# First-layer attention of a decoder: the order of work in one turn, rearranged into two halves on TensorE, ScalarE and VectorE

## The chip, the cores and the metric

One core of a Trainium2 chip runs the whole kernel in one launch. Times are microseconds of that core. A number is the median of several executions or, where a profile is read, belongs to the one execution that was profiled.

## The reference

The kernel computes a two-layer decoder on 4 sequences of 512 tokens with 128 features. Each layer is an attention, a cross-attention and a mixture of experts, each with a layer norm ahead and a residual addition behind. The change lies in the first part of the first layer alone:

```python
q = jnp.einsum('bsf,hfd->bhsd', x, wq)      # x is the layer norm of the input
k = jnp.einsum('bsf,hfd->bhsd', x, wk)
v = jnp.einsum('bsf,hfd->bhsd', x, wv)      # B = 4, S = 512, H = 16 heads of DK = 64
scores = jnp.einsum('bhsd,bhtd->bhst', q, k) / sqrt(DK)
attn = jax.nn.softmax(scores, axis=-1)
out = jnp.einsum('bhst,bhtd->bhsd', attn, v)
x = x_in + out.transpose(0, 2, 1, 3).reshape(B, S, H * DK) @ wo
```

The later parts, among them the second layer's attention with relative positions, are computed by other lines of the same program (`a1_...`), after this one.

## The kernel before, in words

The kernel is written by hand: each engine has its own program, all of them meet through semaphores, and each engine works strictly through its list. Nothing but the written order and the waits decides when a thing runs.

**Turns.** The first attention is a loop of 32 turns. Turn g is one pair of heads of one sequence (8 pairs by 4 sequences). A turn has four query tiles p of 128 tokens, and in each tile two heads, so eight units u = 0 to 7, where u = 2p + head. The first turn, the second and the last are written apart (`first`, `second`, `last`); those between run in a loop of two turns, since buffers with the index `par` alternate.

**What TensorE does in turn g** (`a0_turn` in the tensor block, line 1035):
- `a0_scores(g, p)`, line 991: six matmuls of 64 rows by 512 columns. Queries and keys are each split into a high and a low part, and three products of parts are added, for two heads. The heads lie in the two halves of the rows and run in pairs. They write banks 0 and 1 for even tiles, 2 and 3 for odd ones. Tile p waits for the exponentials that read these banks last (`a0_exp`).
- `a0_turn_t(g, u)`, line 1006: the transposes of unit u's probabilities, four of 128 by 128, into bank 4 for even u, bank 5 for odd. It waits for the normalisation of unit u (`a0_norm`) and for the copy of the unit that was in its bank before (`a0_tcd`, VectorE, or `a0_tca`, ScalarE). The transposes of units 4 to 7 are made in the turn after.
- `a0_values(g - 1, half)`, line 1014: 16 matmuls of 64 columns each that make half of the previous turn's output in bank 7. It needs all copies of that half, and its first half waits until the addition before it has read the bank (`a0_x`).
- `a0_project_q`, `_k`, `_v` of turn g + 1, lines 973 to 989. All three write bank 6, so K waits until Q has been read by both readers (`a0_ql`), V until K has (`a0_kl`), and the next Q until V has (`a0_vc`).
- `a0_output(g - 1)`, line 1028: the product with `wo`, from the copied features (`a0_ftc`) into bank 7.

**What the others do.** VectorE takes the negated maximum of every unit's scores (`a0_maximum`, line 1569), copies even units' transposes (`a0_copy`, 1564), takes the reciprocal of the sum (`a0_reciprocal`, 1578), makes the low parts of Q and K (`a0_low_q`, `a0_low_k`, 1582 to 1589) and adds the output to X (`a0_add`, 1573). ScalarE makes the exponentials (`a0_exp_of`, 737) with the sum in an accumulator, and waits for the transpose of the unit four before, whose probabilities lie in the same buffer; it copies the odd units' transposes (`a0_copy`, 732), Q, K and V out of bank 6 (716 to 726) and the features out of bank 7 (728). GpSimd multiplies each unit's probabilities by the reciprocal (563), in the order of units. SP copies the next pair's weights and the layer norm's output into `wst` and `hst` once the V projection is done (line 417), 32 times; in the first eight turns it also issues the loads of later weights.

**The order before.** TensorE's turn has four equal steps. With (u) for a transpose, those of 4 to 7 and the values belonging to the turn before:

```
p=0: scores 0, (4), (5), values 0, Q     p=1: scores 1, (6), (7), K
p=2: scores 2, (0), (1), values 1        p=3: scores 3, (2), (3), V, output
```

Of the kernel before, what the change touches and what calls it, by code (L numbers as in the profile page):

```python
# [23 lines left out]
QT = SEQ // P  # L24
# [77 lines left out]
def decoder_kernel(nc, a, out):  # L102
    ctx = ExitStack()
    with ctx:
# [254 lines left out]
        PAIRS = B * HP  # L359
        STACK = 16 * 3 * HQ  # L360
        UN = 2 * QT
# [321 lines left out]
        def _(act):  # L683
# [32 lines left out]
            def a0_copy_q(g, par):  # L716
                act.wait_ge(a0_q, g + 1)
                act.activation(a0_qk[par][:, 0, :], bank[6][:, :], ACT.Copy, scale=float(DK) ** -0.5).then_inc(a0_qc, 1)  # L718

            def a0_copy_k(g, par):  # L720
                act.wait_ge(a0_k, g + 1)
                act.activation(a0_qk[par][:, 2, :], bank[6][:, :], ACT.Copy).then_inc(a0_kc, 1)

            def a0_copy_v(g, par):
                act.wait_ge(a0_v, g + 1)
                act.activation(a0_vtok[par], bank[6][:, :].rearrange("p (a b) -> p a b", a=QT), ACT.Copy).then_inc(a0_vc, 1)

            def a0_copy_feats(g):
                act.wait_ge(a0_pv, g * 2 + 2)
                act.activation(featsT[:, :], bank[7][:, :], ACT.Copy).then_inc(a0_ftc, 1)  # L730

            def a0_copy(g, u, par):
                act.wait_ge(a0_t, g * UN + u + 1)
                act.activation(a0_pT[par][1][:, :, (u // 2) * P:(u // 2 + 1) * P],
                               bank[5][:, :].rearrange("p (a b) -> p a b", a=QT), ACT.Copy).then_inc(a0_tca, 1)

            def a0_exp_of(g, u, first):
                act.wait_ge(a0_max, g * UN + u + 1)
                if not (first and u < 4):
                    act.wait_ge(a0_t, g * UN + u - 3)  # L740
                act.activation(a0_p[u % 4], bank[u % 4][:, :], ACT.Exp, bias=negmax[:, u:u + 1],  # L741
                               accum_out=den[:, u:u + 1]).then_inc(a0_exp, 1)

            def a0_turn(g, par, first, last):
                for p in range(QT):
                    a0_exp_of(g, 2 * p, first)
                    a0_exp_of(g, 2 * p + 1, first)
                    if p < 2:
                        if not first:
                            a0_copy(g - 1, 2 * p + 5, 1 - par)  # L750
                    else:
                        a0_copy(g, 2 * p - 3, par)
                    if not last:
                        if p == 0:
                            a0_copy_q(g + 1, 1 - par)
                        if p == 1:
                            a0_copy_k(g + 1, 1 - par)
                        if p == 3:
                            a0_copy_v(g + 1, 1 - par)
                    if p == 2 and not first:  # L760
                        a0_copy_feats(g - 1)

            a0_copy_q(0, 0)
            a0_copy_k(0, 0)
# [183 lines left out]
        def _(pe):  # L948
# [31 lines left out]
            def a0_project_k(g):  # L980
                pe.wait_ge(a0_ql, g + 1)
                pe.matmul(bank[6][:, :], wst[:, 1, :], hst[:, :], start=True, stop=True).then_inc(a0_k, 1)
# [8 lines left out]
            def a0_scores(g, p, par, first):  # L991

                if p == 0:
                    pe.wait_ge(a0_ql, g + 1)
                    pe.wait_ge(a0_kl, g + 1)
                if not (first and p < 2):
                    pe.wait_ge(a0_exp, g * UN + 2 * p - 2)
                for i, (q, k) in enumerate(((0, 2), (0, 3), (1, 2))):
                    for h in range(2):
                        r = h * DK  # L1000
                        mm = pe.matmul(bank[2 * (p % 2) + h][:, :], a0_qk[par][r:r + DK, q, p * P:(p + 1) * P],  # L1001
                                       a0_qk[par][r:r + DK, k, :], start=(i == 0), stop=(i == 2))
                        if i == 2:
                            mm.then_inc(a0_s, 1)
# [28 lines left out]
                mm.then_inc(a0_o, 1)  # L1033

            def a0_turn(g, par, first, last, second=False):
                for p in range(QT):
                    a0_scores(g, p, par, first)
                    for u in (2 * p - 4, 2 * p - 3):
                        if u >= 0:
                            a0_turn_t(g, u, first)  # L1040
                        elif not first:
                            a0_turn_t(g - 1, u + UN, False)
                    if p == 0:
                        if not first:
                            a0_values(g - 1, 1 - par, 0, second)
                        if not last:
                            a0_project_q(g + 1)
                    if p == 1 and not last:
                        a0_project_k(g + 1)
                    if p == 2 and not first:  # L1050
                        a0_values(g - 1, 1 - par, 1, second)
                    if p == 3:
                        if not last:
                            a0_project_v(g + 1)
                        if not first:
                            a0_output(g - 1)

            a0_project_q(0)
            a0_project_k(0)
# [5 lines left out]
                a0_turn(i * 2 + 1, 1, False, False)  # L1065
            a0_turn(PAIRS - 2, 0, False, False)
            a0_turn(PAIRS - 1, 1, False, True)
            a0_values(PAIRS - 1, 1, 0, False)
            for u in range(4, UN):
                a0_turn_t(PAIRS - 1, u, False)  # L1070
            a0_values(PAIRS - 1, 1, 1, False)
            a0_output(PAIRS - 1)

# [70 lines left out]
            for t in range(1, NT + 4):  # L1144
# [5 lines left out]
                u = (t - 3) // 2  # L1150
# [330 lines left out]
            with pe.Fori(0, E1 // 2) as i:  # L1481
                for k in range(8):
# [4 lines left out]
                    for hf in range(2):  # L1487
                        u = 2 * k + hf
# [16 lines left out]
        def _(dve):  # L1505
# [82 lines left out]
                dve.wait_ge(a0_kc, g + 1)  # L1588
                dve.tensor_tensor(a0_qk[par][:, 3, :], bank[6][:, :], a0_qk[par][:, 2, :].bitcast(F32), ALU.subtract).then_inc(a0_kl, 1)

            def a0_turn(g, par, first, last):
                for p in range(QT):
                    a0_maximum(g, 2 * p)
                    a0_maximum(g, 2 * p + 1)
                    if p >= 2:
                        a0_copy(g, 2 * p - 4, par)
                    elif not first:
                        a0_copy(g - 1, 2 * p + 4, 1 - par)
                    a0_reciprocal(g, 2 * p)
                    a0_reciprocal(g, 2 * p + 1)  # L1600
                    if not last:
                        if p == 0:
                            a0_low_q(g + 1, 1 - par)
                        if p == 1:
                            a0_low_k(g + 1, 1 - par)
                    if p == 3 and not first:
                        a0_add(g - 1)

            a0_low_q(0, 0)
            a0_low_k(0, 0)  # L1610
            a0_turn(0, 0, True, False)
            with dve.Fori(0, PAIRS // 2 - 1) as i:
                a0_turn(i * 2 + 1, 1, False, False)
                a0_turn(i * 2 + 2, 0, False, False)
            a0_turn(PAIRS - 1, 1, False, True)
            a0_copy(PAIRS - 1, 4, 1)
            a0_copy(PAIRS - 1, 6, 1)
            a0_add(PAIRS - 1)
# [557 lines left out]
```

## Time and profile before

| what | value |
|---|---|
| time, median of 3 (lowest to highest) | 1595.6 us (1595.15 to 1600.68) |
| the profiled execution | 1596.56 us, of which 1594.8 us from its first to its last instruction |
| TensorE matmuls busy | 1379.0 us, 86% of the span |
| TensorE weight loads busy | 959.2 us, 60% |
| VectorE busy | 999.3 us, 63% |
| ScalarE busy | 724.2 us, 45% |
| GpSimd busy | 540.8 us, 34% |
| granted TensorE clock, mean | 0.925 |
| bytes moved | 61.36 MB, mean 38 GB/s |

The first attention runs from 46.6 us (first scores, line 1001) to about 542 us (last output, line 1031), nearly a third of the span. The page's second part shows the span in 40 slices of 39.9 us:

```
PE   4899999999999789714389759989999999949998
DVE  2566666666666677487033338697787778646554
ACT  2566666666666455300023234454654655523222
POOL 1455555555555200100711255432433434121110
PEclk9999999999999999755789879999999999959999
```

Each digit is a tenth of a slice, 9 being 90% or more; the stage is in slices 2 to 14. How to read it: a matmul's printed duration reaches to the modelled end of its result, so matmuls behind each other overlap in print, and their pace is seen in the distances of their starts. A busy share of TensorE near one says that there is always a matmul under way, not that the array works at its peak. What stands in brackets behind a row is idle time of that engine ahead of it, and what released it.

### The profile page before, as it was taken

To read this page: it belongs to the slowest core of one execution; us is meant where nothing else is said; L and a number is where in the kernel's file an instruction comes from. 1 tells how busy PE (TensorE), PEld (TensorE's weight loads), DVE (VectorE), ACT (ScalarE), POOL (GpSimd) and SP (SyncE) were. 2 spreads that over 40 slices of the span, in tenths; PEclk is the share of its full clock that TensorE was granted. 3 is DMA by queue.
4 is the path that set the end of the run, shared out by engine and by line. 5 is a ranking of instruction groups with operands and counts; after the bars stand their busy time and mean duration, and the time that the engine had idled before them with its cause. 6 is when DMAs were issued, how large, how long until landed. Compare 5 with 4: busy or idle time off the path is not lost.

```text
span 1594.8 us, 30921 instructions
## 1 busy us (share of the span) xinstructions
PE 1379.0 (86%) x10918; PEld 959.2 (60%) x10918; DVE 999.3 (63%) x2407; ACT 724.2 (45%) x1467; POOL 540.8 (34%) x548
## 2 busy tenths in 40 slices
PE   4899999999999789714389759989999999949998
PEld 2566666666666456512167436666766776638887
DVE  2566666666667677487033338697787778646554
ACT  2566666666666455300023234454654655523222
POOL 1455555555555200100711255432433434121110
PEclk9999999999999999755789879999999999959999
DMA  3333011010010200000023123211111211000000
GB/s 131 96 95 109 24 34 35 23 35 33 24 35 23 60 1 1 1 1 1 16 73 91 29 58 108 44 46 30 39 48 29 46 45 41 7 0 1 0 0 26
DMA packets 91918, 61.36 MB, mean 38 GB/s; under 512 B 26841, under 2 KB 78890, under 8 KB 91830
## 3 DMA queue, kind: packets, MB, share of 16 engines
q1 hardware_dynamic: 89782, 58.88, 13.3%
q0 software_dynamic: 2048, 1.27, 0.3%
q8 instruction: 59, 0.97, 0.2%
q14 instruction: 29, 0.24, 0.0%
HBM read 21.63 MB, written 10.49 MB: 20 GB/s over the span
## 4 chain that ended last, share of the span: by engine, by line
PE 75%; DVE 15%; issue 3%; ACT 3%; another core or an unknown queue 2%; SPq 1%; DMA 1%; POOL 0%; DVEq 0%; ACTq 0%
PE psum L1011 8%; PE psum L1024 8%; PE psum L1001 7%; PE psum L1372 7%; PE psum L1494 6%; PE psum L1363 5%; PE psum L1384 4%; PE psum L1476 4%; PE psum L1357 3%; PE psum L1219 2%; PE psum L978 2%; PE psum L987 2%; DVE negmax L1987 2%; PE psum L1031 2%
## 5 line engine op out<-in xcount | busy, mean ns | idle before, releaser
L563 POOL TENSOR_TENSOR arena<-arena,rden 128x512 f32<-128x512 f32 x256 | 260.8, 1040 | 255.3 <-DVE rden L1580 255.3
L741 ACT ACTIVATE arena<-psum,negmax 128x512 f32<-128x512 f32 x256 | 173.6, 683 | 136.0 <-DVE negmax L1571 134.8
L1987 DVE TENSOR_REDUCE negmax<-psum 128x1 f32<-128x512 f32 x256 | 165.2, 685 | 75.9 <-PE psum L1363 69.4
L1571 DVE TENSOR_REDUCE negmax<-psum 128x1 f32<-128x512 f32 x256 | 164.3, 683 | 11.1 <-PE psum L1001 7.5
L1011 PE MATMUL psum<-cst,arena 128*128 128x128 f32 x1024 | 144.0, 280 | 1.6 <-DVE arena L1566 0.7
L1011 PEld LDWEIGHTS psum<-cst,arena 128*128 128x128 f32 x1024 | 109.0, 141 | 53.0 <-issue 51.5
L1001 PE MATMUL psum<-a_qk 64*128 64x512 f32 x768 | 124.5, 429 | 0.0
L1363 PE MATMUL psum<-w,wqkv 128*64 128x208 f32 x1024 | 124.0, 364 | 0.0
L623 POOL TENSOR_TENSOR a_qblk<-a_qstack,cst 96x512 fp32r<-96x512 f32 x64 | 68.6, 1073 | 136.7 <-PE psum L1363 127.8
L1357 PE MATMUL psum<-a_kstack,a_qblk 96*128 96x512 f32 x256 | 97.8, 464 | 16.7 <-DMA a_kstack<-a_klo 16.7
L1001 PEld LDWEIGHTS psum<-a_qk 64*128 64x128 f32 x768 | 62.8, 186 | 69.9 <-issue 59.1
L894 ACT ACTIVATE kT<-psum,negmax 128x512 f32<-128x512 f32 x64 | 44.0, 687 | 125.3 <-PE psum L1372 84.7
L1494 PE MATMUL psum<-f_h,f_w 128*128 128x512 f32 x384 | 99.2, 407 | 1.5 <-DVE arena L2075 0.8
L1363 PEld LDWEIGHTS psum<-w,wqkv 128*64 128x64 f32 x1024 | 64.5, 141 | 58.3 <-issue 48.8
L1991 DVE COPY arena<-psum 128x512 f32<-128x512 f32 x128 | 87.1, 680 | 2.3 <-PE psum L1372 2.3
L894 ACT ACTIVATE hst<-psum,negmax 128x512 f32<-128x512 f32 x64 | 44.0, 687 | 94.6 <-PE psum L1372 47.1
L931 ACT ACTIVATE arena<-psum 128x512 f32<-128x512 f32 x64 | 38.2, 597 | 104.3 <-PE psum L1494 104.3
L1494 PEld LDWEIGHTS psum<-f_h,f_w 128*128 128x128 f32 x384 | 70.5, 191 | 18.9 <-DVE arena L2075 3.5
L888 ACT ACTIVATE arena<-psum 128x512 f32<-128x512 f32 x128 | 76.1, 595 | 1.6 <-PE psum L1372 1.6
L2075 DVE TENSOR_TENSOR arena<-psum,arena 128x512 f32<-128x512 f32 x64 | 44.2, 691 | 47.4 <-ACT arena L931 47.3
L1384 PE MATMUL psum<-arena,w 128*32 128x128 f32 x2048 | 65.5, 276 | 4.5 <-issue 3.6
L1584 DVE SCALAR_TENSOR_TENSOR a_qk<-psum,a_qk 128x512 fp32r<-128x512 f32 x32 | 22.1, 691 | 74.2 <-ACT a_qk L718 74.2
(303 smaller groups left out, 2779.8 us busy)
## 6 DMA issues: line engine op xcount, KB each, us to landing
hst<-hT SPq DMA_DIRECT2D x32, 256.0 KB, 2.3
a_kstack<-a_khi SPq DMA_DIRECT2D x128, 64.0 KB
wst<-wqkv SPq DMA_DIRECT2D x32, 192.0 KB, 2.4
w<-in_ew SPq DMA_DIRECT2D x2, 2048.0 KB, 8.6
a_kstack<-a_klo SPq DMA_DIRECT2D x64, 64.0 KB
xs_rows<-f SPq DMA_DIRECT2D x3, 1024.0 KB, 5.6
arena<-xs_rows SPq DMA_DIRECT2D x8, 384.0 KB, 3.7
ys_rows<-wqkv SPq DMA_DIRECT2D x8, 384.0 KB, 2.7
```

The source lines that it names most:

```text
L563: pool.tensor_tensor(a0_p[u % 4], a0_p[u % 4], rden[:, u:u + 1].broadcast_to([P, SEQ]), ALU.mult).then_inc(a0_norm, 1)
L741: act.activation(a0_p[u % 4], bank[u % 4][:, :], ACT.Exp, bias=negmax[:, u:u + 1], accum_out=den[:, u:u + 1]).then_inc(a0_exp, 1)
L1001: mm = pe.matmul(bank[2 * (p % 2) + h][:, :], a0_qk[par][r:r + DK, q, p * P:(p + 1) * P], a0_qk[par][r:r + DK, k, :], start=(i == 0), stop ...
L1011: mm = pe.transpose(bank[4 + u % 2][:, kt * P:(kt + 1) * P], a0_p[u % 4][:, kt * P:(kt + 1) * P], ident)
L1024: mm = pe.matmul(bank[7][h * DK:(h + 1) * DK, qs], a0_vtok[par][:, kt, h * DK:(h + 1) * DK], a0_pT[par][h][:, kt, qs], start=(kt == 0), st ...
L1357: pe.matmul(bank[n % 4][:, :], qblk[:, hg, j, lg:lg + 2, :, :].rearrange("p g h l -> p (g h l)"), kstack[it % 2][:, n // 4, :], start=True ...
L1363: mm = pe.matmul(bank[n % 4][blk * HQ * LG:(blk + 1) * HQ * LG, first_key:first_key + WIN], rblk[:, hg, j, g, :, :].rearrange("p h l -> p ...
L1372: mm = pe.transpose(bank[4 + n % 2][:, kt * P:(kt + 1) * P], ptile[n % 4][:, kt * P:(kt + 1) * P], ident)
L1384: mm = pe.matmul(bank[6][32 * j:32 * j + 32, grp * P:(grp + 1) * P], vst[:, kt, hg * HG + grp * 4 + j, :], a1_pT(hg, kt, grp, j), start=(k ...
L1494: mm = pe.matmul(bank[2 * (u % 2) + w][:, :], w_parts[:, e, wp, w * FF + hf * P:w * FF + (hf + 1) * P], h_parts[hp][:, c * SEQ:(c + 1) * S ...
L1571: dve.tensor_reduce(negmax[:, u:u + 1], bank[u % 4][:, :], AX.X, ALU.max, negate=True).then_inc(a0_max, 1)
L1987: dve.tensor_reduce(negmax[:, n % 8:n % 8 + 1], bank[n % 4][:, :], AX.X, ALU.max, negate=True).then_inc(a1_max, 1)
```

## The change

The bodies of the three turns are written out anew, with the same instructions in another order. Scores of tiles 0 and 1 follow each other, and so do those of tiles 2 and 3. Transposes, values and projections stand between these pairs:

```
first half:  scores 0, scores 1, output of turn g-2, (4), (5), values 0, Q, (6), (7), K
second half: scores 2, scores 3, (0), (1), values 1, (2), (3), V
```

The output and the addition to X are a turn later than before, behind the first two score tiles; two outputs come behind the last turn, and there the transposes 4 and 5 precede the first half of the values, 6 and 7 the second. ScalarE's and VectorE's orders follow. ScalarE's is now exponentials 0, 1, copy 5, Q, exponentials 2, 3, copy 7, K, exponential 4, copy 1, exponential 5, features, exponential 6, copy 3, exponential 7, V. VectorE's loop now also has the second turn written apart. GpSimd's and SP's programs are not changed. The helper functions that issue instructions are not changed either.

```diff
--- before.py
+++ after.py
@@ -742,23 +742,28 @@
                                accum_out=den[:, u:u + 1]).then_inc(a0_exp, 1)
 
             def a0_turn(g, par, first, last):
-                for p in range(QT):
-                    a0_exp_of(g, 2 * p, first)
-                    a0_exp_of(g, 2 * p + 1, first)
-                    if p < 2:
-                        if not first:
-                            a0_copy(g - 1, 2 * p + 5, 1 - par)
-                    else:
-                        a0_copy(g, 2 * p - 3, par)
-                    if not last:
-                        if p == 0:
-                            a0_copy_q(g + 1, 1 - par)
-                        if p == 1:
-                            a0_copy_k(g + 1, 1 - par)
-                        if p == 3:
-                            a0_copy_v(g + 1, 1 - par)
-                    if p == 2 and not first:
-                        a0_copy_feats(g - 1)
+                a0_exp_of(g, 0, first)
+                a0_exp_of(g, 1, first)
+                if not first:
+                    a0_copy(g - 1, 5, 1 - par)
+                if not last:
+                    a0_copy_q(g + 1, 1 - par)
+                a0_exp_of(g, 2, first)
+                a0_exp_of(g, 3, first)
+                if not first:
+                    a0_copy(g - 1, 7, 1 - par)
+                if not last:
+                    a0_copy_k(g + 1, 1 - par)
+                a0_exp_of(g, 4, first)
+                a0_copy(g, 1, par)
+                a0_exp_of(g, 5, first)
+                if not first:
+                    a0_copy_feats(g - 1)
+                a0_exp_of(g, 6, first)
+                a0_copy(g, 3, par)
+                a0_exp_of(g, 7, first)
+                if not last:
+                    a0_copy_v(g + 1, 1 - par)
 
             a0_copy_q(0, 0)
             a0_copy_k(0, 0)
@@ -1033,27 +1038,31 @@
                 mm.then_inc(a0_o, 1)
 
             def a0_turn(g, par, first, last, second=False):
-                for p in range(QT):
-                    a0_scores(g, p, par, first)
-                    for u in (2 * p - 4, 2 * p - 3):
-                        if u >= 0:
-                            a0_turn_t(g, u, first)
-                        elif not first:
-                            a0_turn_t(g - 1, u + UN, False)
-                    if p == 0:
-                        if not first:
-                            a0_values(g - 1, 1 - par, 0, second)
-                        if not last:
-                            a0_project_q(g + 1)
-                    if p == 1 and not last:
-                        a0_project_k(g + 1)
-                    if p == 2 and not first:
-                        a0_values(g - 1, 1 - par, 1, second)
-                    if p == 3:
-                        if not last:
-                            a0_project_v(g + 1)
-                        if not first:
-                            a0_output(g - 1)
+                a0_scores(g, 0, par, first)
+                a0_scores(g, 1, par, first)
+                if not (first or second):
+                    a0_output(g - 2)
+                if not first:
+                    a0_turn_t(g - 1, 4, second)
+                    a0_turn_t(g - 1, 5, second)
+                    a0_values(g - 1, 1 - par, 0, second)
+                if not last:
+                    a0_project_q(g + 1)
+                if not first:
+                    a0_turn_t(g - 1, 6, second)
+                    a0_turn_t(g - 1, 7, second)
+                if not last:
+                    a0_project_k(g + 1)
+                a0_scores(g, 2, par, first)
+                a0_scores(g, 3, par, first)
+                a0_turn_t(g, 0, first)
+                a0_turn_t(g, 1, first)
+                if not first:
+                    a0_values(g - 1, 1 - par, 1, second)
+                a0_turn_t(g, 2, first)
+                a0_turn_t(g, 3, first)
+                if not last:
+                    a0_project_v(g + 1)
 
             a0_project_q(0)
             a0_project_k(0)
@@ -1065,9 +1074,12 @@
                 a0_turn(i * 2 + 1, 1, False, False)
             a0_turn(PAIRS - 2, 0, False, False)
             a0_turn(PAIRS - 1, 1, False, True)
+            a0_output(PAIRS - 2)
+            a0_turn_t(PAIRS - 1, 4, False)
+            a0_turn_t(PAIRS - 1, 5, False)
             a0_values(PAIRS - 1, 1, 0, False)
-            for u in range(4, UN):
-                a0_turn_t(PAIRS - 1, u, False)
+            a0_turn_t(PAIRS - 1, 6, False)
+            a0_turn_t(PAIRS - 1, 7, False)
             a0_values(PAIRS - 1, 1, 1, False)
             a0_output(PAIRS - 1)
 
@@ -1588,31 +1600,46 @@
                 dve.wait_ge(a0_kc, g + 1)
                 dve.tensor_tensor(a0_qk[par][:, 3, :], bank[6][:, :], a0_qk[par][:, 2, :].bitcast(F32), ALU.subtract).then_inc(a0_kl, 1)
 
-            def a0_turn(g, par, first, last):
-                for p in range(QT):
-                    a0_maximum(g, 2 * p)
-                    a0_maximum(g, 2 * p + 1)
-                    if p >= 2:
-                        a0_copy(g, 2 * p - 4, par)
-                    elif not first:
-                        a0_copy(g - 1, 2 * p + 4, 1 - par)
-                    a0_reciprocal(g, 2 * p)
-                    a0_reciprocal(g, 2 * p + 1)
-                    if not last:
-                        if p == 0:
-                            a0_low_q(g + 1, 1 - par)
-                        if p == 1:
-                            a0_low_k(g + 1, 1 - par)
-                    if p == 3 and not first:
-                        a0_add(g - 1)
+            def a0_turn(g, par, first, last, second=False):
+                a0_maximum(g, 0)
+                a0_maximum(g, 1)
+                if not (first or second):
+                    a0_add(g - 2)
+                a0_maximum(g, 2)
+                a0_maximum(g, 3)
+                if not first:
+                    a0_copy(g - 1, 4, 1 - par)
+                a0_reciprocal(g, 0)
+                a0_reciprocal(g, 1)
+                if not last:
+                    a0_low_q(g + 1, 1 - par)
+                if not first:
+                    a0_copy(g - 1, 6, 1 - par)
+                a0_reciprocal(g, 2)
+                a0_maximum(g, 4)
+                a0_reciprocal(g, 3)
+                a0_maximum(g, 5)
+                a0_copy(g, 0, par)
+                if not last:
+                    a0_low_k(g + 1, 1 - par)
+                a0_maximum(g, 6)
+                a0_maximum(g, 7)
+                a0_reciprocal(g, 4)
+                a0_reciprocal(g, 5)
+                a0_copy(g, 2, par)
+                a0_reciprocal(g, 6)
+                a0_reciprocal(g, 7)
 
             a0_low_q(0, 0)
             a0_low_k(0, 0)
             a0_turn(0, 0, True, False)
-            with dve.Fori(0, PAIRS // 2 - 1) as i:
+            a0_turn(1, 1, False, False, second=True)
+            with dve.Fori(1, PAIRS // 2 - 1) as i:
+                a0_turn(i * 2, 0, False, False)
                 a0_turn(i * 2 + 1, 1, False, False)
-                a0_turn(i * 2 + 2, 0, False, False)
+            a0_turn(PAIRS - 2, 0, False, False)
             a0_turn(PAIRS - 1, 1, False, True)
+            a0_add(PAIRS - 2)
             a0_copy(PAIRS - 1, 4, 1)
             a0_copy(PAIRS - 1, 6, 1)
             a0_add(PAIRS - 1)
```

## Rows read from the trace of the kernel before

**Rows 1.** Chain that ended last, shares by line, from the page.

```profile
PE psum L1011 8%; PE psum L1024 8%; PE psum L1001 7%; PE psum L1372 7%; PE psum L1494 6%; PE psum L1363 5%; PE psum L1384 4%; PE psum L1476 4%; PE psum L1357 3%; PE psum L1219 2%; PE psum L978 2%; PE psum L987 2%; DVE negmax L1987 2%; PE psum L1031 2%
```

**Rows 2.** Windows view; busy of PE, PEld, DVE, ACT, POOL; clock; DMA.

```profile
250.00:300.00 50.00, 50.00 (x352) 32.25 (x352) 34.16 (x76) 31.80 (x78) 26.12 (x26) 1.00 0.08 28
```

**Rows 3.** Chain in order of time, first and last of 53 pieces.

```profile
109.10 1.88 PE psum L1024 x16
...
505.60 1.88 PE psum L1024 x16
```

**Rows 4.** Timeline, TensorE, one turn; start us, us, what.

```profile
306.21 1.09 PE L1011 MATMUL psum<-cst,arena 128*128 128x128 f32 x8
307.24 1.95 PE L1024 MATMUL psum<-arena,vtok 128*64 128x256 f32 x16
309.11 1.12 PE L978 MATMUL psum<-hst,wst 128*128 128x512 f32 x2
310.17 0.97 PE L1001 MATMUL psum<-a_qk 64*128 64x512 f32 x6
311.07 1.09 PE L1011 MATMUL psum<-cst,arena 128*128 128x128 f32 x8
312.00 1.02 PE L982 MATMUL psum<-hst,wst 128*128 128x512 f32 x2
312.95 0.96 PE L1001 MATMUL psum<-a_qk 64*128 64x512 f32 x6
...
318.74 1.06 PE L987 MATMUL psum<-wst,hst 128*128 128x128 f32 x8
319.63 1.06 PE L1031 MATMUL psum<-wqkv,featsT 128*128 x8
320.62 0.96 PE L1001 MATMUL psum<-a_qk 64*128 64x512 f32 x6
```

**Rows 5.** Timeline, TensorE, narrow windows that begin inside a group.

```profile
310.50 0.63 PE L1001 MATMUL psum<-a_qk 64*128 64x512 f32 x4
310.74 0.40 PE L1001 MATMUL psum<-a_qk 64*128 64x512 f32 x2
...
311.23 0.93 PE L1011 MATMUL psum<-cst,arena 128*128 128x128 f32 x7
```

**Rows 6.** Timeline, all engines, the stage's first turn.

```profile
50.16 1.10 PE L978 MATMUL psum<-hst,wst 128*128 128x512 f32 x2 [2.04 <-issue]
...
51.29 0.60 ACT L718 ACTIVATE a_qk<-psum 128x512 fp32r<-128x512 f32 x1 [0.97 <-PE psum L978]
51.92 0.69 DVE L1584 SCALAR_TENSOR_TENSOR a_qk<-psum,a_qk 128x512 fp32r<-128x512 f32 x1 [1.40 <-ACT a_qk L718]
52.74 0.50 PEld L982 LDWEIGHTS psum<-hst,wst 128*128 128x128 f32 x2 [0.65 <-DVE a_qk L1584]
```

**Rows 7.** Timeline, a steady turn's addition, then the last turn.

```profile
320.90 0.69 DVE L1576 TENSOR_TENSOR X<-X,psum 128x512 f32 x1 [0.62 <-PE psum L1031]
...
532.13 0.67 DVE L1576 TENSOR_TENSOR X<-X,psum 128x512 f32<-128x512 f32 x1
...
532.95 1.95 PE L1024 MATMUL psum<-w,arena 128*64 128x256 f32 x16 [1.22 <-DVE X L1576]
...
534.83 1.09 PE L1011 MATMUL psum<-cst,arena 128*128 128x128 f32 x8
535.52 0.69 DVE L1566 COPY w<-psum 128x512 f32<-128x512 f32 x1 [2.72 <-PE psum L1011]
```

**Rows 8.** Timeline, ScalarE, a steady turn.

```profile
313.07 0.68 ACT L741 ACTIVATE arena<-psum,negmax 128x512 f32<-128x512 f32 x1
313.64 0.20 ACT L741 ACTIVATION_READ_ACCUMULATOR arena<-psum,negmax 128x1 f32 x1
313.73 0.60 ACT L734 ACTIVATE arena<-psum 128x512 f32<-128x512 f32 x1
314.21 0.60 ACT L722 ACTIVATE a_qk<-psum 128x512 fp32r<-128x512 f32 x1
```

## The prediction

> **What bounds the kernel now.** I read the shares of the chain that ended last first: three of its largest entries, lines 1011, 1024 and 1001, are TensorE lines of the first layer's attention, the only stage that the diff touches [rows 1]. The second layer's attention with relative positions is in later lines, which the diff leaves alone: its cost is nothing, and a change that was meant for it has not been made there. The next view is the busy time in a stretch of the stage: TensorE is busy for all 50 us at a granted clock of 1.00, VectorE, ScalarE and GpSimd for 34, 32 and 26 [rows 2]. So the stage runs at TensorE's own pace. The chain's pieces give that pace: the first and the last of 53 values groups, two to a turn, lie 396.50 us apart, which is 26 turns of 15.25 us [rows 3].
>
> The timeline of one turn shows what the pace is made of [rows 4]. I write S for the six score matmuls of a query tile, T for the transposes of two units (head and tile), V for a half of the values, Q, K and P for the projections of query, key and value, O for the output; T(u) is unit u's transpose. What counts is the step from the start of one group to the start of the next; the printed durations overlap. S is 0.90, T 0.93 ahead of K and 1.03 ahead of V, V 1.87, Q 1.06, K 0.95, P 0.89, O 0.99.
>
> **A change of form costs time.** S uses 64 rows of the array, V 64 columns, all others the whole [rows 4]. P and O are eight equal matmuls each, and only O is followed by another form: leaving costs 0.10. Q and K do the same work, both leave, and only Q follows another form: entering costs 0.11. Narrow views of S and T say the same: the pairs of S start 0.33, 0.24 and 0.33 apart (the last to the T behind), so 0.09 goes at each end, and T's first step is 0.16 where the seven behind it take 0.77, or 0.11 each: entering costs T 0.05 [rows 5]. Entering V was part of V before and still is.
>
> **The turn without waits.** The new order is S S O T V Q T K, S S T V T P. It has eight changes of form, the old one eleven.
> - S S: 0.33 + 4 x 0.24 + 0.33 = 1.62, taken as 1.61 since 0.24 is rounded up; twice 3.22. Two separate pairs cost 3.60 before.
> - O behind S: 0.89 + 0.11 = 1.00. T(4), T(5) behind O, ahead of V: 8 x 0.11 + 0.10 = 0.97.
> - V 1.87 twice; the one step from V to T that rows show, 532.95 to 534.83, is 1.88 [rows 7], so I take 1.88.
> - Q ahead of T, no leaving: 0.96. T(6), T(7) between Q and K: 0.87. K 0.95.
> - T(0), T(1) between S and V 1.03; T(2), T(3) behind V 0.93; P, now leaving to S, 0.99.
> The sum is 3.22 + 1.00 + 0.97 + 3.76 + 0.96 + 0.87 + 0.95 + 1.03 + 0.93 + 0.99 = 14.68, which is 0.57 less than 15.25. Were that all, the change would give back 17 us. No arithmetic is added or removed, no DMA; SP's staging starts behind P as before; O, S, T and V lay between P's end and Q, 4.8 us, now S S O T V do, 5.5, so its two DMAs land no later relative to Q.
>
> **The wait at K.** K writes the bank of Q, so it waits until ScalarE has copied Q and VectorE has taken the low part. In the old turn S and T stand between Q and K: 312.00 - 309.11 = 2.89 [rows 4]. In the new one only T(6), T(7) do: 0.96 + 0.87 = 1.83. What the chain needs is seen in the kernel's first turn, where too little stood between them: Q starts at 50.16, the copy at 51.29, the low part at 51.92, and the load for K at 52.74, its idle time put down to that low part: 2.58 [rows 6]. TensorE stands for 0.75, and K has a cold start, worth an entry, 0.11: 0.86 a turn. It isn't hidden: all that stands behind K in the queue, the whole second half, moves with it. On ScalarE the copy of Q now stands ahead of the exponentials of units 2 and 3, on VectorE the low part ahead of copy 6; they have until the second half, over 2 us later.
>
> **The wait at V.** The output moved to follow the scores, and the values behind it write the bank that VectorE's addition to X reads. Addition starts 1.27 after a warm O starts [rows 4, 7], so 1.38 after one that enters; from its start to the values it releases is 0.82 (532.13 to 532.95) [rows 7]. Needed 2.20, filled by O and T 1.97: 0.23 a turn. In VectorE's queue the maxima of units 2 and 3 stand behind this addition and come 1 us later than they could; the score tiles that need their banks are 5 us off. Before, the addition had four groups' time and cost nothing.
>
> **The wait at the second S.** It writes the banks of units 6 and 7, so it needs exponential 7. That reuses unit 3's probabilities and stands in ScalarE's queue behind exponential 6, which needs T(2), and copy 3. From T(2)'s start: 0.69 to its first reader (534.83 to 535.52) [rows 7], then 0.66 from an exponential to a copy, 0.48 from a copy to the next, 0.77 to the end of the accumulator's read [rows 8], 0.13 from an end to TensorE's start (52.61 to 52.74) [rows 6]: 2.73. TensorE needs 0.93 + 0.99 + 0.81 for T, P and the first S: 2.73 too. Between 0 and 0.3 (were a step slower, with the cold start); I take 0.05, nearer the lower end, as every step is measured.
>
> Other releases come early by this reckoning: GpSimd's normalisations, 26 of 50 us busy [rows 2], get units 0 to 3 over 2 us ahead of their transposes; exponentials 0 and 1 now wait for T(4) and T(5) until about 3 us into the turn, and what needs them comes after 9.
>
> **The sum.** 14.68 + 0.86 + 0.23 + 0.05 = 15.82, so 0.57 a turn longer; over 29 steady turns +16.5. The ends: turn 1 has no O and no addition to wait for, 1.23 less, so -0.7 against before; the first turn takes its second S earlier, -0.4; the tail has its transposes ahead of the values, so that copies run beside them, an estimate of -1.1. Together +14.3. The profiled execution took 1596.56 (span 1594.8): 1610.9. It stands 1.0 over the median of 1595.6, so for a median I say 1610.
>
> **The rivals.** A change of this kernel can be told from none from about 0.5%, 8 us, on.
> - Forecast: the K wait and most of the two others, 1604 to 1616. Chance 0.60.
> - Only K waits, or the drains saved are some tenths larger: 14.68 + 0.86 = 15.54, 29 x 0.29 - 2.2 = +6, so 1602. For it: the addition's start rests on one latency, and the last wait is even. Against: the addition is a plain chain of measured steps. Chance 0.14.
> - Faster: the Q to K chain is covered after all, and only the drains count. It decides at K: with the other waits in place the turn is equal to the old one when Q to K takes about 2.0, and 1.83 with no other wait gives -17 and the ends: 1577. For it: TensorE is the only full engine [rows 2] and three changes of form are really gone. Against: 2.58 is measured with ScalarE and VectorE idle ahead of the two steps [rows 6], and nothing in the diff shortens a step. Chance 0.09.
> - The last wait grows: the exponentials of the second half have only T(2) to P to run in, and if a ScalarE step there takes 0.3 more, with it every turn: +9, so 1619. For it: the sum is even, with no slack. Chance 0.12.
> - The two S side by side save nothing, since the second tile's weights can't load while both row halves still stream: then each joint costs what it did, 0.18, or 0.36 a turn, and the time is 1620. Against: inside S the third pair's loads are hidden at 0.24 with both halves in flight [rows 5]. Chance 0.05. The Trainium skill, "TensorE: Matmul & The Clock Gate", Part 3, states a rule for it: weight loads overlap matmuls in flight only where the row group differs. By that rule 0.24 could not be; the trace doesn't agree inside a group, and at a joint no row shows it.
>
> **How the numbers follow.** The time is the forecast's. The range of 1600 to 1618 takes in the K-only case and the forecast's bounds; outside are the covered chain and the upper parts of the last two. Slower by over 0.5%: forecast, the grown wait, the joint, 0.77; within: 0.14; faster: 0.09.
>
> **What would show it.** In the changed profile: turns of about 15.8, two score groups as one of x12 over 1.6 us; idle time of TensorE of about 0.75 ahead of line 982's matmuls, put down to the low part of Q, and about 0.2 ahead of the first values, put down to the addition; busy below 50 of 50 in the stretch, clock still 1.00; lines of later stages unchanged. No idle time at K, or a turn under 15.3, proves me wrong.

## The result, and the profile after

The changed kernel takes 1608.3 us, the median of 13 runs (1603.82 to 1616.56), the kernel before 1595.6 us, the median of 13 (1590.78 to 1603.16). The ratio is 1.0072, with a 95% interval of 1.0054 to 1.0089: slower by 12.7 us. The forecast was 1610, in 1600 to 1618.

The chain in order of time of the changed kernel, the first and the last of 51 values groups, answers to [rows 3]:

```profile
104.83 1.88 PE psum L1029 x16
...
500.28 1.88 PE psum L1029 x16
```

They lie 395.45 us apart, which is 25 turns of 15.82 us. Before it was 15.25, and 15.82 was forecast. The busy time in the stretch of [rows 2] (columns as there):

```profile
250.00:300.00 50.00, 47.83 (x345) 32.74 (x344) 31.69 (x73) 31.95 (x78) 27.04 (x28) 1.00 0.08 28
```

TensorE is no longer busy throughout, its clock is still 1.00, and it issues 345 matmuls in 50 us where it issued 352. The timeline of TensorE over one turn, answering to [rows 4]:

```profile
300.10 1.16 PE L1036 MATMUL psum<-wqkv,featsT 128*128 x8
301.09 1.04 PE L1016 MATMUL psum<-cst,arena 128*128 128x128 f32 x8
302.32 1.95 PE L1029 MATMUL psum<-w,arena 128*64 128x256 f32 x16 [0.19 <-DVE X L1588]
304.20 1.12 PE L983 MATMUL psum<-hst,wst 128*128 128x512 f32 x2
305.16 1.04 PE L1016 MATMUL psum<-cst,arena 128*128 128x128 f32 x8
306.74 1.13 PE L987 MATMUL psum<-hst,wst 128*128 128x512 f32 x2 [0.54 <-DVE a_qk L1596]
307.79 1.66 PE L1006 MATMUL psum<-a_qk 64*128 64x512 f32 x12
309.39 1.09 PE L1016 MATMUL psum<-cst,arena 128*128 128x128 f32 x8
310.41 1.95 PE L1029 MATMUL psum<-w,arena 128*64 128x256 f32 x16
312.29 1.09 PE L1016 MATMUL psum<-cst,arena 128*128 128x128 f32 x8
313.22 1.06 PE L992 MATMUL psum<-wst,hst 128*128 128x128 f32 x8
314.20 1.79 PE L1006 MATMUL psum<-a_qk 64*128 64x512 f32 x12
315.92 1.16 PE L1036 MATMUL psum<-wqkv,featsT 128*128 x8
```

Three places are to be seen, in the letters of the prediction.
- **K.** From T(6), T(7) at 305.16 to K at 306.74 it is 1.58 where the transposes alone take 0.87: TensorE stands for 0.71, and its idle time is put down to VectorE's low part of Q. K's own step is 1.05 (306.74 to 307.79), 0.10 over a warm K's 0.95. Together 0.81.
- **V.** From T(4), T(5) at 301.09 to the values at 302.32 it is 1.23, against 0.97 without a wait: 0.26, put down to the addition to X.
- **The second S.** The pair of tiles at 314.20 takes 1.72 to the next group, the pair at 307.79 takes 1.60: 0.12.

The sum is 1.19 us a turn, and 15.82 - 1.19 leaves 14.63 for a turn without waits, 0.62 less than the old turn of 15.25. About 0.5 of it comes of fewer changes of form and of scores side by side, the rest of a short wait in the old turn, shown further down. The waits take it all and more. The timeline of the other engines shows the chain behind K's wait, answering to [rows 6]:

```profile
305.36 0.60 ACT L718 ACTIVATE a_qk<-psum 128x512 fp32r<-128x512 f32 x1 [1.69 <-PE psum L983]
...
305.99 0.69 DVE L1596 SCALAR_TENSOR_TENSOR a_qk<-psum,a_qk 128x512 fp32r<-128x512 f32 x1 [1.89 <-ACT a_qk L718]
...
306.74 0.30 PEld L987 LDWEIGHTS psum<-hst,wst 128*128 128x128 f32 x2 [0.78 <-DVE a_qk L1596]
```

Q starts at 304.20, K at 306.74: 2.54, where the first turn of the kernel before took 2.58. ScalarE and VectorE both stood idle ahead of their step, so neither is late: it is the chain itself that is long. And the last wait, on the load side of TensorE and on ScalarE:

```profile
314.20 0.69 ACT L741 ACTIVATE arena<-psum,negmax 128x512 f32<-128x512 f32 x1
314.77 0.21 ACT L741 ACTIVATION_READ_ACCUMULATOR arena<-psum,negmax 128x1 f32 x1
...
315.03 0.53 PEld L1006 LDWEIGHTS psum<-a_qk 64*128 64x128 f32 x6 [0.27 <-ACT arena L741]
```

Exponential 7 starts at 314.20, its accumulator is read by 314.98, and the loads for the second tile start at 315.03, 0.83 behind the first tile.

**Where the stage ends.** The last output of the kernel before and of the changed one, each a line of TensorE's timeline (the window of the second ends before the last of its eight matmuls):

```profile
540.83 1.16 PE L1031 MATMUL psum<-wqkv,featsT 128*128 128x128 f32 x8 [0.69 <-ACT featsT L730]
```

```profile
557.12 1.05 PE L1036 MATMUL psum<-wqkv,featsT 128*128 128x128 f32 x7 [0.69 <-ACT featsT L730]
```

The stage ends 16.3 us later. The profiled execution took 1616.56 us, the highest of the 13 and 20.0 more than the one before, so 3.7 came later. They lie in one stretch of the second layer's attention, here in the windows view of the kernel before and then of the changed one:

```profile
1100.00:1120.00 20.00, 19.79 (x185) 13.84 (x183) 15.65 (x34) 11.27 (x20) 7.01 (x7) 1.00 0.20 50
```

```profile
1116.00:1136.00 20.00, 19.79 (x147) 13.31 (x145) 12.88 (x27) 8.48 (x14) 3.75 (x4) 0.74 0.20 50
```

The same work ran at a mean granted clock of 0.74 instead of 1.00, so half of that stretch at the lower of the two levels, and got through 147 matmuls instead of 185. The change touches nothing there, and runs of one and the same kernel lie up to 13 us apart. I read totals to some 4 us, therefore, and turns to hundredths.

### The profile page after: what moved, and what is told of

Its sections match the earlier page's. It is cut to its first block, busy times and chain, and to the rows that moved or that the text cites. A ratio compares the mean times of both kernels' runs of the same rounds, so it can differ in the third digit from the quotient of the medians.

```text
span 1614.8 us, 30925 instructions
## 1 busy us (share of the span) xinstructions
PE 1377.8 (85%) x10918; PEld 976.0 (60%) x10918; DVE 994.3 (62%) x2407; ACT 728.8 (45%) x1467; POOL 541.5 (34%) x548
## 4 chain that ended last, share of the span: by engine, by line
PE 72%; DVE 17%; ACT 3%; issue 3%; another core or an unknown queue 2%; SPq 1%; DMA 1%; DVEq 0%; POOL 0%; ACTq 0%
PE psum L1029 8%; PE psum L1384 7%; PE psum L1006 7%; PE psum L1506 6%; PE psum L1375 5%; PE psum L1016 4%; PE psum L1396 4%; PE psum L1488 4%; PE psum L1369 3%; PE psum L987 2%; PE psum L983 2%; PE psum L1231 2%; PE psum L1036 2%; DVE negmax L2014 2%; PE psum L992 2%
## 5 line engine op out<-in xcount | busy, mean ns | idle before, releaser
L1016 PEld LDWEIGHTS psum<-cst,arena 128*128 128x128 f32 x1024 | 113.6, 141 | 41.4 <-issue 39.8
L1016 PE MATMUL psum<-cst,arena 128*128 128x128 f32 x1024 | 136.6, 276 | 0.4 <-DVE arena L1578 0.4
L1006 PE MATMUL psum<-a_qk 64*128 64x512 f32 x768 | 113.0, 424 | 0.3 <-ACT arena L741 0.3
L1006 PEld LDWEIGHTS psum<-a_qk 64*128 64x128 f32 x768 | 66.3, 189 | 47.1 <-ACT arena L741 32.6
L626 POOL TENSOR_TENSOR wqkv<-big_k,cst 128x512 f32<-128x512 f32 x64 | 67.6, 1056 | 0.0
```

The source lines that it names most:

```text
L1016: mm = pe.transpose(bank[4 + u % 2][:, kt * P:(kt + 1) * P], a0_p[u % 4][:, kt * P:(kt + 1) * P], ident)
```

## The experiments

Each turn length below is read from the chain as above, from two of its values groups a whole number of turns apart. Times are medians, each beside runs of the kernel before on the same chip. The turns came out within 0.1 us of what was expected, but for K ahead of transposes (0.25 more). All eight totals came out above, by 2.5 to 8 us. Against the kernel before, they differ from 29 times the change of the turn by 1.1 less to 4.4 more, so the theories are judged by the turns.

### The price of a change of form

The kernel before, with the V projection between the two halves of the second values group:

```diff
                 for kt in range(QT):
+                    if kt == 2 and between:
+                        between()
                     for h in range(2):
...
-                        a0_values(g - 1, 1 - par, 1, second)
+                        a0_values(g - 1, 1 - par, 1, second, None if last else lambda: a0_project_v(g + 1))
                     if p == 3:
-                        if not last:
+                        if first:
                             a0_project_v(g + 1)
```

> The kernel before with the V projection put between the two halves of the 16 matmuls of the second values group, so that two changes of form are added (values to projection, projection to values) and no instruction and no wait. Theory (a change of form costs 0.15 to 0.2 us): turn 15.25 + 0.36 = 15.6 us, time 1595.6 + 11 = 1607. Rival (form costs nothing, what is saved by side-by-side scores is something of the scores alone): 15.25 us, 1596.

1611.2 us, ratio 1.0076 (1.0046 to 1.0106). The chain, 24 turns apart, then TensorE's timeline:

```profile
108.23 1.88 PE psum L1026 x16
...
482.49 1.88 PE psum L1026 x16
```

```profile
303.00 1.08 PE L1026 MATMUL psum<-w,arena 128*64 128x256 f32 x8
304.01 1.16 PE L987 MATMUL psum<-wst,hst 128*128 128x128 f32 x8
305.10 1.08 PE L1026 MATMUL psum<-w,arena 128*64 128x256 f32 x8
306.12 0.96 PE L1001 MATMUL psum<-a_qk 64*128 64x512 f32 x6
```

The turn is 15.59 us, 0.34 more: 0.17 for each of two changes, with no new wait. The parts show it: the two halves of V take 1.01 and 1.02, together 0.15 over one V of 1.88, and P takes 1.09, 0.20 over its 0.89. The rival that form costs nothing falls.

### The wait at K, made in the kernel before

The same wait without anything else of the change: K ahead of transposes 6 and 7 instead of behind them.

```diff
                 for p in range(QT):
                     a0_scores(g, p, par, first)
+                    if p == 1 and not last:
+                        a0_project_k(g + 1)
                     for u in (2 * p - 4, 2 * p - 3):
...
-                    if p == 1 and not last:
-                        a0_project_k(g + 1)
```

> The kernel before with the key projection ahead of transposes 6 and 7 instead of behind them, nothing else. Theory: Q to K takes 2.6 us, and only Q and one score tile, 1.96 us, stand between them, so TensorE stands for 0.64 with about 0.05 for the cold start: turn 15.25 + 0.69 = 15.9 us, time 1595.6 + 31 x 0.69 = 1617. Rival (the transposes' own short waits, 0.13 us a turn, are absorbed by it): 15.8, 1613. Rival (the K wait is hidden): 15.25, 1596.

1624.9 us, ratio 1.0158 (1.0115 to 1.0200). TensorE's timeline:

```profile
210.70 0.96 PE L1001 MATMUL psum<-a_qk 64*128 64x512 f32 x6
212.18 1.12 PE L982 MATMUL psum<-hst,wst 128*128 128x512 f32 x2 [0.52 <-DVE a_qk L1584]
...
215.00 0.66 PE L1011 MATMUL psum<-cst,arena 128*128 128x128 f32 x4
215.86 0.63 PE L1011 MATMUL psum<-cst,arena 128*128 128x128 f32 x4 [0.20 <-ACT w L734]
```

The turn is 16.15 us (24 turns from 127.08 to 514.68 in its chain), 0.90 more, where I had 0.69. The K wait is near the expected 0.64: 1.48 from S to K instead of 0.90, 0.58. The rest is mostly a wait that I had expected to be absorbed: T(7) moved 0.96 nearer to T(1), which needs its bank, and the copy between them stands on ScalarE behind two exponentials. T(0), T(1) take 1.42 here (215.00 to 216.42), 1.18 and 1.11 in two turns of the kernel before, and 1.03 with no wait. A K wait in an otherwise old turn costs what the chain says, and a moved group also moves what its bank's next user waits for.

### K behind the scores, in the changed kernel

```diff
-                if not last:
-                    a0_project_k(g + 1)
                 a0_scores(g, 2, par, first)
                 a0_scores(g, 3, par, first)
+                if not last:
+                    a0_project_k(g + 1)
```

> The changed kernel with the key projection moved from ahead of the scores of tiles 2 and 3 to behind them. Theory (the K wait costs 0.8 us a turn because too little stands between Q and K): TensorE's idle time ahead of K is gone, but the third-tile scores then reach exponential 3 early. That exponential stands behind the copy of Q: in the changed kernel's trace the load of Q starts at 304.20, exponential 3 starts at 306.52 and its read ends at 307.30, 3.1 us behind Q, while tile 3's scores would now come 2.7 us behind it. So a wait of about 0.5 with a cold start takes the place of the 0.8: turn about 15.5 us against 15.82, time about 1599. Rival (the copy and the low part are hidden and the turn is long for another reason): turn stays at 15.8, 1608. Rival (nothing takes its place): turn 15.0, 1584.

1605.5 us, ratio 1.0052 (1.0029 to 1.0075). TensorE's timeline:

```profile
312.45 0.97 PE L1006 MATMUL psum<-a_qk 64*128 64x512 f32 x6
313.67 0.96 PE L1006 MATMUL psum<-a_qk 64*128 64x512 f32 x6 [0.26 <-ACT arena L741]
```

The turn is 15.58 (24 turns from 121.64 to 495.64 in its chain), 0.24 less than the changed kernel's. K no longer waits, and tile 3's scores do: 1.22 from tile 2's instead of the 0.81 of three unstalled pairs, put down to an exponential. So 0.81 was removed and 0.57 came back in its place. 0.51 of that is this wait and its restart (tiles 2 and 3 take 2.11, where an unstalled pair takes 1.60), since exponential 3 stands behind the copy of Q on ScalarE; the other 0.06 is K's entry, which is dearer than the transposes'. The K wait hid this one in the changed kernel.

### The output back at the end of the turn

```diff
-                if not (first or second):
-                    a0_output(g - 2)
...
                 if not last:
                     a0_project_v(g + 1)
+                if not first:
+                    a0_output(g - 1)
```

The addition goes with it, to the end of VectorE's turn.

> The changed kernel with the output and the addition to X back at the end of the turn, behind the V projection. Theory (the values wait for the addition 0.24 us a turn, the second score tile 0.1 for exponential 7, and the output behind scores pays an entry of 0.06 more than a transpose does): idle time ahead of the first values goes, the second tile's scores come 0.9 us later behind exponential 7 and don't wait, the K wait stays at 0.8. Turn 15.82 - 0.24 - 0.12 - 0.05 = 15.4 us, time about 1597. Rival (these are small and the K wait takes up whatever they give): turn 15.8, 1608.

1603.1 us, ratio 1.0037 (1.0014 to 1.0060).

The turn is 15.38 (24 turns from 138.06 to 507.26 in its chain), 0.44 less than the changed kernel's; 0.26 of it is the wait for the addition, 0.12 the one for exponential 7, the rest the warmer entries. The K wait was untouched: Q to K takes 2.54 (309.08 to 311.62 in its timeline). The place of the output and the place of Q each cost by themselves.

### Exponential 7 ahead of copy 3

```diff
                 a0_exp_of(g, 6, first)
-                a0_copy(g, 3, par)
                 a0_exp_of(g, 7, first)
+                a0_copy(g, 3, par)
```

> The changed kernel with exponential 7 ahead of copy 3 on ScalarE, nothing else. Theory (the second score tile waits for exponential 7, 0.12 us a turn with its restart): the chain from T(2) to the end of exponential 7 is shorter by a copy's step of 0.48, so the wait goes: turn 15.82 - 0.12 = 15.70 us, time 1608 - 4 = 1604. Rival (the later copy 3 makes transpose 5 or the V copy late): turn 15.8 or more, 1608. Nothing changes at K or at the first values.

The second pair of tiles in TensorE's timeline:

```profile
308.98 1.66 PE L1006 MATMUL psum<-a_qk 64*128 64x512 f32 x12
310.56 1.16 PE L1036 MATMUL psum<-wqkv,featsT 128*128 x8
```

The turn is 15.68 (24 turns from 124.59 to 500.94 in its chain), 0.14 less, and the pair takes 1.58 instead of 1.72: the wait is named rightly. The total doesn't show it: 1611.2 us, ratio 1.0087 (1.0065 to 1.0110), overlaps with that of the changed kernel. 4 us are less than what the rest of the kernel varies by.

### Q ahead of the values: the version that keeps the gain

If both large waits come of too little work behind a start, one move mends both: Q one place earlier puts V behind Q, and puts Q between O and V.

```diff
                     a0_turn_t(g - 1, 5, second)
-                    a0_values(g - 1, 1 - par, 0, second)
                 if not last:
                     a0_project_q(g + 1)
+                if not first:
+                    a0_values(g - 1, 1 - par, 0, second)
```

> The changed kernel with the query projection one place earlier on TensorE, behind transposes 4 and 5 and ahead of the first values. Theory (both large waits come of too little work behind a start): between Q and K then stand V, T(6) and T(7), 3.8 us against the 2.6 needed, and between O and V stand T and Q, 2.9 against 2.2, so both waits go. The changes of form stay eight. Exponential 3 ends about 6.1 us behind the transposes' start, tile 3's scores come at 6.5. Turn 14.63 + 0.12 for the second score tile = 14.75 us, time 1595.6 - 30 x 0.5 - 2 = 1578. Rival: Q now stands 3.6 us behind the end of the V projection, and the copy of the layer norm's output into its buffer lands about 3.5 us behind it; if it lands later, Q waits for the DMA, 0.2 to 0.5 us a turn: 15.1, 1587. Rival (stalls elsewhere take it back): 15.8, 1608.

1580.5 us, ratio 0.9882 (0.9832 to 0.9932) against the kernel before. With exponential 7 first as well:

> Q ahead of the first values and exponential 7 ahead of copy 3, both edits on the changed kernel. Theory: no wait of TensorE's is left in the turn, 14.63 us, time about 1575. Rivals: Q waits for its DMA, 0.2 to 0.5 us, 1581 to 1590; or exponential 3 for tile 3's scores.

1581.3 us, ratio 0.9896 (0.9855 to 0.9937). Part of the second one's turn:

```profile
301.72 1.07 PE L983 MATMUL psum<-hst,wst 128*128 128x512 f32 x2
302.72 1.95 PE L1029 MATMUL psum<-arena,vtok 128*64 128x256 f32 x16
304.60 1.09 PE L1016 MATMUL psum<-cst,arena 128*128 128x128 f32 x8
305.53 1.02 PE L987 MATMUL psum<-hst,wst 128*128 128x512 f32 x2
306.48 1.66 PE L1006 MATMUL psum<-a_qk 64*128 64x512 f32 x12
```

The turns are 14.72 (23 turns from 137.09 to 475.54 in its chain) and 14.63 us (23 turns from 141.81 to 478.33), and in the second none of these groups has idle time ahead of it. Q ahead of the values is enough: the total falls from the 1595.8 us that the kernel before took beside it, by 15 us, and beats both kernels. The last version has Q ahead of the values and the output at the end of the turn, with exponential 7 where the changed kernel has it:

> Q ahead of the first values, and the output and the addition at the end of the turn instead of behind the scores. Theory: eight changes of form as well, but O enters behind P in its own form and T(4) behind scores, which is 0.06 less, and the second score tile has 0.9 us more behind exponential 7: no wait is left, turn 14.57 us, time about 1574. If the turn with O behind the scores is as long as this one, the place of the output doesn't matter once Q is early. Rival: Q's DMA, as it starts with the end of P, has the same 3.6 us: 0.2 to 0.5 us, 1580 to 1589.

1580.8 us, ratio 0.9888 (0.9844 to 0.9933), a turn of 14.63 (23 turns from 137.59 to 474.07 in its chain). I had 14.57. The turn is 0.09 shorter than with Q ahead of the values alone, as the second score tile no longer waits (1.60 for the pair instead of 1.72), and as long as with exponential 7 first; in the total none of this can be seen. Its timeline shows where the next limit lies:

```profile
311.10 1.09 PE L1016 MATMUL psum<-cst,arena 128*128 128x128 f32 x8
312.06 1.10 PE L983 MATMUL psum<-hst,wst 128*128 128x512 f32 x2
313.09 1.95 PE L1029 MATMUL psum<-w,arena 128*64 128x256 f32 x16
```

Q takes 1.03 here, and 0.95 with Q ahead of the values alone (312.67 to 313.62 there). SP issued the copy of the layer norm's output at 309.64, and these land 2.3 us after their issue (median), at about 311.9, just ahead of Q. That points to the rival of Q's DMA, at some 0.1 us a turn and not at 0.2 to 0.5; the profile names no release for it, so it isn't shown.

## Why the prediction was right

**The turn without waits, 14.68.** Worked out from the steps of groups in their old neighbourhoods, it came out as 14.63 (15.82 less the three waits). The changes of form are what this rests on, and the kernel before with two of them added paid 0.17 each. P's share of that, 0.20, had been read as 0.21, an entry and a leaving; for the values' share, 0.15, the prediction had no price. Its steps for the old turn add up to 15.15, though, and not to 15.25. The rest is a wait of the kernel before that it didn't see, at T(0), T(1):

```profile
313.85 1.26 PE L1011 MATMUL psum<-cst,arena 128*128 128x128 f32 x8
315.03 1.95 PE L1024 MATMUL psum<-arena,vtok 128*64 128x256 f32 x16
```

The step is 1.18 where 1.03 was taken, and 1.11 in the turn after. ScalarE's copy out of T(1)'s bank ends at 314.33 [rows 8], and T(1)'s weight loads start at 314.44 in the timeline. So 0.1 of the 0.57 that the order was to save was a wait and not form. The forecast of the new turn doesn't suffer, as it is a sum of steps without waits.

**The wait at K, 0.86.** Measured 0.81, by the chain that was read in the kernel's first turn: 2.58 there, 2.54 here. The hand-back from VectorE, 0.13 there, is 0.06 here (306.68 to 306.74); the windows view grants TensorE a mean clock of 0.50 from 52 to 54 us of the kernel before, where the 0.13 was read. This was the largest term and decided the sign.

**The wait at V, 0.23.** Measured 0.26. Needed were 2.20 from O's start to V, and it is 2.22 (300.10 to 302.32).

**The second S, 0.05.** Measured 0.12. Chain and filling came out nearly even, 2.74 (312.29 to 315.03) against 2.72, and the wait itself is 0.02: the second tile starts 0.83 behind the first where three pairs take 0.81. That the chain came within 0.01 is partly luck: the hand-back was 0.05 and not 0.13, and the step to exponential 6 (0.75 from T(2)'s start) and the one to copy 3 (0.68) were longer than the 0.69 and 0.66 taken. The other 0.10 is the restart. I had set the restart against the whole range and not against its lower end.

**The ends, -2.2.** This was the term that was off. 29 turns at 0.57 are 16.5, and the stage ended 16.3 later, so the ends gave 0.2 instead of 2.2. I had put the first turn at -0.4; in the profiled execution the second turn starts at 62.11 instead of 60.39, 1.5 later once the 0.2 that the stage itself began later is taken off. Against the forecast -0.4 that is the whole miss, as the other ends gave 1.9, near the 1.8 forecast. The first turn's projections in TensorE's timeline, answering to [rows 6]:

```profile
50.40 2.04 PE L983 MATMUL psum<-hst,wst 128*128 128x512 f32 x2 [0.62 <-issue]
53.86 2.07 PE L987 MATMUL psum<-hst,wst 128*128 128x512 f32 x2 [1.41 <-DVE a_qk L1596]
```

Q took 2.04 where it had taken 1.10, and K steps on after 2.00 where 0.95 is usual (K did so in the kernel before as well: 1.99, from 52.74 to 54.73): twice as long, as at the lower of the clock's two levels. The windows view grants that stretch the full clock. The same view of the version with Q and exponential 7 moved, whose first turn has the same order and nearly the same durations, follows and says half:

```profile
50.00:57.00 7.00, 5.19 (x10) 1.94 (x12) 2.06 (x6) 3.24 (x9) 3.08 (x3) 1.00 0.50 145
```

```profile
50.00:57.00 7.00, 5.22 (x10) 1.97 (x12) 2.04 (x6) 3.21 (x9) 3.07 (x3) 0.50 0.51 144
```

So the pace of the matmuls is to be trusted over the record here. Nor is the slow first turn the rule for this order: with exponential 7 first, and everything else as in the changed kernel, Q and K ran at full pace:

```profile
50.43 1.10 PE L983 MATMUL psum<-hst,wst 128*128 128x512 f32 x2 [1.35 <-issue]
52.94 1.12 PE L987 MATMUL psum<-hst,wst 128*128 128x512 f32 x2 [1.41 <-DVE a_qk L1596]
```

There the second turn starts at 59.19, 1.2 ahead of the kernel before. And a version with the old order, the one with P inside the values, had the slow Q too (2.04). What makes the clock late in one execution and not in another isn't shown.

**The total.** 1610 forecast, 1608.3 measured, within what the rest of the kernel varies by. The sign and the 0.57 a turn are earned; that the total is within 2 us is luck. The ends that were forecast weren't there in the profiled execution, and the medians lie 12.7 apart where 29 turns make 16.5.

**The rivals.** That only K waits falls: V and the second S are named in the trace, and two runs removed them. That the K chain is covered falls. That the last wait grows falls at 0.12. That side-by-side scores save nothing falls too. Narrow windows of the changed kernel's timeline, each beginning inside the pair of tiles at 307.79, show the joint:

```profile
308.36 1.09 PE L1006 MATMUL psum<-a_qk 64*128 64x512 f32 x8
...
308.60 0.86 PE L1006 MATMUL psum<-a_qk 64*128 64x512 f32 x6
...
308.82 0.63 PE L1006 MATMUL psum<-a_qk 64*128 64x512 f32 x4
```

The second tile starts with six matmuls left, at 308.60, 0.24 behind the pair ahead of it and 0.22 ahead of the next: the same step as inside a tile. The rule of the Trainium skill ("TensorE: Matmul & The Clock Gate", Part 3) that weight loads overlap matmuls in flight only where the row group differs would have asked for more at the joint, since both row groups were streaming. The trace doesn't agree with it there either.

## What to carry to other kernels

Where one engine is full and works through a list, an order is judged by two sums: what the list costs by itself, changes of array form included, and for each hand-over and back to another engine, whether the work in between is longer than that chain. Both can be read before a line is written, the second from a place in the old trace where the chain was bare, such as a first or a last turn. Grouping alike work shortens the first sum and thins out the cover of the second; starting the long chain one group earlier gave the cover back here, and turned 12.7 us of loss into 15 us of gain.

## What the hardware showed that I hadn't expected

A wait of TensorE doesn't always end with its release: K behind a stall of 0.71 cost 0.10 more than a warm one, and a stall of 0.02 at the second S cost the same 0.10 again. The load side shows what is lost. In the kernel before K's weight load starts 0.11 ahead of its matmul at 312.00:

```profile
311.89 0.30 PEld L982 LDWEIGHTS psum<-hst,wst 128*128 128x128 f32 x2
```

In the changed kernel, behind the wait, both start at 306.74. Where the form changes anyway there is no such lead to lose: the values behind the addition's wait take 1.88 (302.32 to 304.20), as those without a wait do (310.41 to 312.29), and K behind scores in the kernel before with K early takes 0.96 (212.18 to 213.14) behind its wait, as K behind the scores in the changed kernel does without one (314.56 to 315.52). So a restart and an entry look like one cost, paid once; I read that from these four places and no run tests it by itself.

And a chain over two other engines is steady as long as Q itself runs at its full pace: Q to K took 2.58 in the first turn of one kernel and 2.54 in the middle of another. In the slow first turn of the changed kernel it took 3.46 (50.40 to 53.86), as Q itself took twice as long.
